# Last batch of a memory-attention kernel: result rows staged in four buffers, and the last head's share added to a result prepared without it

## What is computed

```python
xn = layernorm(x)
# attention memory: 8 heads, chunks of 64 tokens, weights updated by scanned gradients
vals = silu(q @ (mem_w0 + updates0)) @ (mem_w1 + updates1)      # per head, 128 wide
vals = rmsnorm(vals) * (mh_gamma + 1.0) * sigmoid(sr @ w_gate)  # scale per token and head
s = (vals of all heads side by side) @ w_combine                # a sum over heads
# top-1 expert of 8 for each token
ffn = relu(xln @ w1[e] + b1[e]) @ w2[e] + b2[e]
g = silu(xn + alpha * ffn)
out = x + s * g                                                 # s is shifted by 63 tokens
```

## Time and profile before

| | us |
|---|---|
| median of 3 runs | 1113.71 |
| lowest and highest run | 1113.23, 1114.35 |
| the profiled execution: its own time | 1113.32 |
| its span, first to last instruction | 1110.8 |
| mean granted TensorE clock in the span, share of full speed | 0.987 |

### The profile page before, as it was taken

The page is one execution under the profiler, slowest core; times in us unless marked ns, Lnnn a source line. Parts: engine busy times, 40 slices in busy tenths (PEclk is TensorE's granted clock), DMA queues, the critical chain, the costliest instruction groups (busy, mean ns, idle before and its releaser), DMA issues. The chain is left out here.

```text
span 1110.8 us, 19052 instructions
## 1 busy us (share of the span) xinstructions
PE 1071.7 (96%) x6613; PEld 900.1 (81%) x6613; DVE 686.0 (62%) x1752; ACT 678.7 (61%) x1356; POOL 562.4 (51%) x574
## 2 busy tenths in 40 slices
PE   6899799999999999999999999999999999999994
PEld 4666588888888888888888888888888888888883
DVE  5887566767766555565556555565556555657774
ACT  5776466677655656565556555665566565656663
POOL 6885244478874444344434444444434443444553
PEclk9999699999999999999999999999999999999997
DMA  7210300000030000000000000000000000012221
GB/s 205 79 46 29 105 1 1 1 15 30 21 97 12 19 10 9 8 21 10 9 8 11 20 11 8 9 20 11 8 8 11 20 8 6 6 42 61 69 70 42
DMA packets 42129, 32.66 MB, mean 29 GB/s; under 512 B 4042, under 2 KB 36652, under 8 KB 41900
## 3 DMA queue, kind: packets, MB, share of 16 engines
q1 hardware_dynamic: 38484, 25.93, 8.0%
q0 software_dynamic: 2304, 4.74, 1.3%
q10 hardware_dynamic: 1248, 0.79, 0.2%
HBM read 18.30 MB, written 13.41 MB: 29 GB/s over the span
## 5 line engine op out<-in xcount | busy, mean ns | idle before, releaser
L1040 DVE TENSOR_TENSOR p_sb<-bank,coef 128x512 f32<-128x512 f32 (+3 forms) x512 | 218.8, 483 | 3.1 <-PE bank L749 2.6
L1232 POOL TENSOR_TENSOR sq_rest<-sq,sq_high 128x450 f32<-128x450 f32 x64 | 67.2, 1050 | 245.1 <-ACT sq_high L934 245.1
L772 PE MATMUL bank<-p_sb,err_t 128*128 128x450 f32 (+3 forms) x512 | 132.9, 402 | 0.2 <-DVE p_sb L1040 0.2
L772 PE MATMUL bank<-p_sb,du_t 128*128 128x450 f32 (+3 forms) x512 | 128.8, 394 | 0.0
L772 PEld LDWEIGHTS bank<-p_sb,err_t 128*128 128x128 f32 x512 | 83.7, 190 | 45.5 <-DVE p_sb L1040 25.2
L1236 POOL TENSOR_TENSOR sq_low<-sq_rest,sq_mid 128x450 bf16<-128x450 f32 x64 | 67.6, 1056 | 96.5 <-ACT sq_mid L948 96.2
L772 PEld LDWEIGHTS bank<-p_sb,du_t 128*128 128x128 f32 x512 | 82.1, 190 | 41.4 <-issue 23.9
L1093 DVE SCALAR_TENSOR_TENSOR acc<-bank,rg,acc 128x128 f32<-128x128 f32 x224 | 62.9, 343 | 68.2 <-POOL rg L1220 68.2
L1118 DVE SCALAR_TENSOR_TENSOR du<-q_sb,bank 128x512 f32<-128x512 f32 x64 | 44.0, 688 | 87.7 <-PE bank L749 87.7
L1216 POOL TENSOR_TENSOR rs<-ms,neg_half 128x4 f32<-128x4 f32 x64 | 80.6, 1259 | 28.6 <-DVE ms L1075 27.3
L1207 POOL TENSOR_TENSOR s_low<-s_sb,s_high 128x512 fp32r<-128x512 f32 x64 | 82.7, 1293 | 20.2 <-ACT s_high L911 20.1
(11 more groups left out here) (297 smaller groups left out, 3103.1 us busy)
## 6 DMA issues: line engine op xcount, KB each, us to landing
sorted_rows<-coef SPq DMA_DIRECT2D x5, 516.0 KB, 5.0
rows<-sorted_rows SPq DMA_DIRECT2D x40, 64.5 KB, 1.8
x<-in_L_attn_inputs SPq DMA_DIRECT2D x8, 256.0 KB, 5.5
x_rows<-x SPq DMA_DIRECT2D x8, 256.0 KB, 2.3
ew<-in_L_ffn_w SPq DMA_DIRECT2D x8, 256.0 KB, 3.9
attn_out<-acc SPq DMA_DIRECT2D x7, 256.0 KB, 2.1
ew<-attn_out SPq DMA_DIRECT2D x7, 256.0 KB
ew<-ffn_rows SPq DMA_DIRECT2D x8, 192.0 KB
```

Source lines behind the costliest of these rows:

```text
L772: last = pe.matmul(out[:, P * i:QW], rows[:, i, :], p_sb[:, P_COL[i]:P_COL[i] + QW - P * i], start=False, stop=True, skip_group_check=True)
L1040: last = nc.vector.tensor_tensor(dst, src, w, ALU.mult)
L1232: nc.gpsimd.tensor_tensor(sq_rest[:], sq[:], sq_3[0][:], ALU.subtract).then_inc(g_rest, 1)
```

## The change

Five edits, all in `attend`:

1. Four sets of `fin_f`, `fin_x`, `fin_o` in place of two. The odd ones lie in the space of the first expert weights. Semaphores and SP's loop follow: sets 0 to 3 are loaded one behind the other, and set c after result c-4 has been stored.
2. The work on them is placed anew. `SUMMED` says whose `last_sum` comes at the end of which head's step: batch h in head h up to 2, batches 3 and 4 in head 3, then 5, 6, 7 in heads 4, 5, 6, none in head 7. `gate_rows` and POOL's product come in the next head's step, at its end as before (a first of two ahead of `vals`); `add_rows` comes one head later still, and in the middle of the step, between `err_low` (L1115) and `du` (L1118).
3. In the last head's step the squares are not split into three bf16 parts: TensorE multiplies the fp32 `sq` by a column of ones in fp32, four products.
4. In the last head's step VectorE makes batch 7's result but for its last head's share, and `finish` then adds that share alone, in two halves. SP stores the result by two transfers, and ScalarE's queue issues the third.
5. The five operations on the token factors become `shares()`, called at the end of head 2's step.

The diff, cut to its core:

```diff
@@ -30,6 +30,8 @@
...
 X_FIRST, X_LAST = 2, 6
+FINS = 4
+SUMMED = [(0,), (1,), (2,), (3, 4), (5,), (6,), (7,), ()]
@@ -678,7 +680,8 @@
...
         late = carve(m.ew2[:].rearrange("p e k d -> p (e k d)"), [0])
-        fin_f, fin_x, fin_o = ([late(T, D) for k in range(2)] for _ in range(3))
+        later = carve(m.ew1[:].rearrange("p e d -> p (e d)"), [0])
+        fin_f, fin_x, fin_o = ([(late, later)[k % 2](T, D) for k in range(FINS)] for _ in range(3))
@@ -729,9 +732,13 @@
...
-        def last_head(s):
-            return s[1] if s is not None and s[0] == B - 1 else None
+        def summed(s):
+            if s is None or s[0] < B - 1:
+                return (), ()
+            return SUMMED[s[1]], SUMMED[s[1] - 1] if s[1] else ()
+        final = lambda s: s == (B - 1, H - 1)
@@ -862,8 +869,13 @@
...
                             pe.matmul(VB[0:r, t * P:t * P + P], vals[:, t * P:t * P + r], m.w_out[:, s[1], :], start=True, stop=True)
-                        pe.wait_ge(g_lo, k + 1)
-                        for t, r in enumerate(Q_ROWS):
+                        if final(s):
+                            pe.wait_ge(a_sq, k + 1)
+                            for t, r in enumerate(Q_ROWS):
+                                last = pe.matmul(QA[0:r, SUMS + t:SUMS + t + 1], sq[:, t * P:t * P + r], m.ones[:, 0:1], start=True, stop=True)
+                        else:
+                            pe.wait_ge(g_lo, k + 1)
+                        for t, r in enumerate(() if final(s) else Q_ROWS):
@@ -924,6 +936,9 @@
...
                         nc.scalar.copy(err_2[0][:], err[:]).then_inc(a_eh, 1)
+                    begun = summed(s)[1]
+                    for c in begun if final(s) else begun[:-1]:
+                        gate_rows(c)
@@ -931,7 +946,8 @@
...
                         act.wait_ge(a_sq, k + 1)
-                        nc.scalar.copy(sq_3[0][:], sq[:]).then_inc(a_hi, 1)
+                        if not final(s):
+                            nc.scalar.copy(sq_3[0][:], sq[:]).then_inc(a_hi, 1)
@@ -943,12 +959,11 @@
...
                         nc.scalar.copy(du_t[:].rearrange("p t d -> p (t d)"), EB[:]).then_inc(a_dt, 1)
-                    if s is not None:
+                    if s is not None and not final(s):
...
                         nc.scalar.copy(sq_3[1][:], sq_rest[:]).then_inc(a_mid, 1)
-                    c = last_head(s)
-                    if c is not None and c > 0:
-                        gate_rows(c - 1)
+                    if begun and not final(s):
+                        gate_rows(begun[-1])
@@ -959,7 +974,8 @@
...
                     if f is None and s is None:
-                        gate_rows(B - 1)
+                        act.wait_ge(v_o, B + 1)
+                        act.dma_start(out[B - 1, SHIFT + (T - 1) * P:S, :], fin_o[(B - 1) % FINS][0:Q_LAST - 1, T - 1, :]).then_inc(s_res[(B - 1) % FINS], 16)
@@ -1020,6 +1036,9 @@
...
                     nc.vector.tensor_copy(m.xl_all[:, :, D].bitcast(I32), m.token_i[:]).then_inc(v_placed, 1)
+                def shares():
@@ -1085,6 +1104,9 @@
...
                             dve.wait_ge(v_acc, l)
+                    if final(z):
+                        finish()
+                    elif z is not None:
@@ -1113,6 +1135,10 @@
...
                         nc.vector.tensor_tensor(err_2[1][:], err[:], err_2[0][:], ALU.subtract).then_inc(v_el, 1)
+                    for c in summed(z)[1]:
+                        if c < B - 1:
+                            add_rows(c)
+                    if f is not None:
@@ -1131,6 +1157,8 @@
...
                             coefs(1)
+                        if k == 2:
+                            shares()
@@ -1140,18 +1168,15 @@
...
                         dve.wait_ge(m.s_scatter, 16 * NT)
-                    c = last_head(s)
-                    if c is not None:
+                    for c in summed(s)[0]:
                         last_sum(c)
-                        if c > 0:
-                            add_rows(c - 1)
-                    if s is None and f is None:
-                        finish_batch()
+                    if final(s):
+                        attention_before_last_head()
...
-                    q = c % 2
-                    dve.wait_ge(s_fin[q], 16 * 5 * (c // 2 + 1) if c < B - 1 else 16 * (5 * 3 + 4))
+                    q = c % FINS
+                    dve.wait_ge(s_fin[q], 16 * 5 * (c // FINS + 1) if c < B - 1 else 16 * (5 + 4))
@@ -1159,19 +1184,30 @@
...
                 def add_rows(c):
-                    q = c % 2
+                    q = c % FINS
...
-                def finish_batch():
-                    q = (B - 1) % 2
+                def attention_before_last_head():
+                    q = (B - 1) % FINS
                     dve.wait_ge(a_g, B)
-                    dve.wait_ge(v_acc, B * H)
-                    dve.wait_ge(s_res[q], 32 * ((B - 1) // 2))
+                    dve.wait_ge(v_acc, B * H - 1)
+                    dve.wait_ge(s_res[q], 32 * ((B - 1) // FINS))
+                    link(nc.vector.tensor_tensor(fin_o[q], acc[:], fin_f[q], ALU.mult))
+                    link(nc.vector.tensor_tensor(fin_o[q], fin_o[q], fin_x[q], ALU.add))
+                def finish():
+                    q = (B - 1) % FINS
                     for k in range(2):
+                        for t in range(2 * k, 2 * k + 2):
+                            r = Q_ROWS[t]
+                            share = fin_f[q][0:r, t, :]
+                            last = nc.vector.scalar_tensor_tensor(share, VB[0:r, t * P:t * P + P], rg[0:r, t:t + 1], share, ALU.mult, ALU.mult)
+                        link(last)
                         part = lambda t: t[:, 2 * k:2 * k + 2, :]
-                        link(nc.vector.tensor_tensor(part(fin_o[q]), part(acc[:]), part(fin_f[q]), ALU.mult))
-                        nc.vector.tensor_tensor(part(fin_o[q]), part(fin_o[q]), part(fin_x[q]), ALU.add).then_inc(v_o, 1)
+                        nc.vector.tensor_tensor(part(fin_o[q]), part(fin_o[q]), part(fin_f[q]), ALU.add).then_inc(v_o, 1)
@@ -1244,10 +1280,9 @@
...
                         nc.gpsimd.indirect_dma_start(m.ffn_rows, bass.IndirectOffsetOnAxis(ids[r][:, 0:1], axis=0), y[r], None).then_inc(s_y[r], 16)
-                    c = last_head(s)
-                    if c is not None and c > 0:
-                        q = (c - 1) % 2
-                        pool.wait_ge(a_g, c)
+                    for c in summed(s)[1] if not final(s) else ():
+                        q = c % FINS
+                        pool.wait_ge(a_g, c + 1)
@@ -1276,15 +1311,15 @@
...
                 def parts(c):
-                    q = c % 2
+                    q = c % FINS
...
                 def result(c, k=None):
-                    q, src = c % 2, fin_o[c % 2]
-                    for t0, t1 in ((0, T - 1), (T - 1, T)) if k is None else (((0, 2),) if k == 0 else ((2, 3), (3, 4))):
+                    q, src = c % FINS, fin_o[c % FINS]
+                    for t0, t1 in ((0, T - 1), (T - 1, T)) if k is None else ((2 * k, 2 + k),):
@@ -1314,20 +1349,21 @@
...
                 for c in range(B):
-                    if c >= 2:
-                        sp.wait_ge(v_o, c - 1)
-                        result(c - 2)
-                        sp.wait_ge(s_res[c % 2], 32 * (c // 2))
+                    if c >= FINS:
+                        sp.wait_ge(v_o, c - FINS + 1)
+                        result(c - FINS)
+                        sp.wait_ge(s_res[c % FINS], 32 * (c // FINS))
...
                     parts(c)
-                sp.wait_ge(v_o, B - 1)
-                result(B - 2)
+                for c in range(B - FINS, B - 1):
+                    sp.wait_ge(v_o, c + 1)
+                    result(c)
...
                     result(B - 1, k)
-                sp.wait_ge(s_res[0], 32 * B // 2)
-                sp.wait_ge(s_res[1], 32 * B // 2 + 16)
+                for q in range(FINS):
+                    sp.wait_ge(s_res[q], 32 * (B // FINS) + (16 if q == (B - 1) % FINS else 0))
```

More of the change, by code:

```diff
@@ L713, in attend @@
         s_y = [sem(f"s_y{k}") for k in range(RING)]
-        s_fin, s_res = ([sem(f"{n}{k}") for k in range(2)] for n in ("s_fin", "s_res"))
+        s_fin, s_res = ([sem(f"{n}{k}") for k in range(FINS)] for n in ("s_fin", "s_res"))
         v_f, a_g, g_o, v_o = sem("v_f"), sem("a_g"), sem("g_o"), sem("v_o")
@@ L882, in gate_rows @@
                         n = c * T + t
-                        last = nc.scalar.activation(fin_f[c % 2][:, t, :], fin_f[c % 2][:, t, :], ACT.Silu, bias=token_q[:, 1, n:n + 1], scale=token_q[:, 2, n:n + 1])
+                        last = nc.scalar.activation(fin_f[c % FINS][:, t, :], fin_f[c % FINS][:, t, :], ACT.Silu, bias=token_q[:, 1, n:n + 1], scale=token_q[:, 2, n:n + 1])
                     last.then_inc(a_g, 1)
```

## The result

The changed kernel takes 1105.39 us (median of 5 runs, 1102.08 to 1106.67), the kernel before beside it on the same chip 1113.79 (5 runs, 1113.23 to 1114.4). The ratio is 0.992, with a 95% interval of 0.9903 to 0.9936: 8.4 us less, faster, and inside the predicted range of 1104.7 to 1107.6. The profiled execution took 1105.39, with a span of 1103.6, where the kernel before had 1113.32 and 1110.8. So 7.2 us went out of the span, and another 0.7 lies around it (own time less span: 2.5 before, 1.8 after). Lines named here are lines of the changed kernel, and in the experiments of the kernel that was run.

A forecast was written before the change was run, and what follows sets the result against it. TensorE, busy 96% of the span, was taken as the bound. Terms 1.0 + 0.9 + 0.6 + 4.3 + 0.8 + 0.1 = 7.7 us off 1113.32 gave 1105.6, plus 0.39 for the runs' median: 1106.0, range 1104.7 to 1107.6.

The forecast's parts named there:

- Step ends in batch 7: Steps behind heads 1, 2, 5 recover 0.34 us each, heads 3 and 4 stay late; 1.0 us won, bounds 0 to 1.7.
- Token factors: Batch 0: without the five operations at the step's end, ms comes earlier; 0.9 us won, bounds 0.6 to 1.0.
- Start of the last head's step: TensorE waits there for xs_low behind a late ms; all 0.61 comes back: 0.6 us won, bounds 0.5 to 0.65.
- Squares in fp32: Last head's step: vals to ms shrinks from 6.99 to 2.65 us; 4.3 us won, bounds 3.0 to 5.2.
- The last share: Kernel's end: last additions to last add take 2.07 us instead of 2.89; 0.8 us won, bounds 0.6 to 0.9.
- The last transfers: Kernel's end: two issuers let the last transfers end sooner; 0.1 us won, bounds −0.5 to 0.35.
- Step ends stay late: Rival: double sums or POOL hold ms in all five steps of batch 7; 6.7 us won, 1107.0 us; chance 0.11.
- all of them recover: Rival: all step ends recover, last sums being faster; +0.7, 1105.3 us, with cheaper squares 1104.7; chance 0.11.
- the fp32 sums slow: Rival: last head's fp32 sums run at 1.2 GHz or cost double; 1.0 to 1.3 us less won, 1107.2; chance 0.07.
- the prepared result in the way: Rival: in the last step ms queues on VectorE behind the result's preparation; the 4.3 goes, 1110.3 us; chance 0.02.
- Slower: the loads of sets 4 to 7: Rival: last_sum waits for loads that need a stored result, ms behind it; 13.2 us cost, 1119.2 us; chance 0.03.

The follow-up runs named there:

- Experiments 4: The changed kernel with the last head's squares in three bf16 parts again, the rest kept: 1107.37 us, ratio 0.9935.
- 7: The kernel before with only the last head's squares taken in plain fp32: one run, 1111.69 us beside 1111.6 for the kernel before.
- Experiments 1: The changed kernel with one small product on POOL after its last work, which nothing waits for: 1107.79 us, ratio 0.9945.
- 3: The changed kernel with the last head added before products and adds again, and SP issuing all three transfers: 1105.53 us, ratio 0.9924.
- experiment 8: The changed kernel with the last head's root on ScalarE, its reciprocal and product on VectorE, off POOL: one run, 1101.96 us beside 1111.6.
- 11: 10 with the last head added before products and adds again: 1102.38 us, ratio 0.9908.
- 10: The changed kernel with the last head's rs and rg off POOL, one last_sum per head's step, and SP issuing the third transfer: 1102.85 us, ratio 0.9904.
- experiment 6: The changed kernel with three sets of result buffers instead of four: one run, 1111.07 us beside 1111.6 for the kernel before.
- experiment 5: The changed kernel with POOL's product of result rows moved to the middle of the next step: one run, 1107.35 us beside 1111.6.

## Why the prediction was right, and where it was wrong

| term | predicted | measured, us |
|---|---|---|
| Step ends in batch 7 | 1.0 | 1.2 |
| Token factors | 0.9 | 0.86 |
| Start of the last head's step | 0.6 | 0.60 |
| Squares in fp32 | 4.3 | 4.5 |
| The last share | 0.8 | 0 |
| The last transfers | 0.1 | 0 |
| sum | 7.7 | 7.1 (span: 7.2) |

From the first projection to the end it is 985.9 us before and 978.5 after, 7.4 less. The 0.2 beyond the terms lies spread over steps that no edit touches. The token factors and the start of the last head's step have no run of their own; they are read from the rows.

*Step ends in batch 7.* Right in kind: behind heads 1, 2 and 5 all came back, behind heads 3 and 4 not. The four steps took 56.26 us and take 55.40, and `w1n` in the fifth is 0.34 earlier: 1.2. Mis-sized was the step behind head 3, for which I had a loss of 0.48 against 0.34; it lost 0.31 (14.04 less 13.73). `ms` was 0.59 late and not 0.75: the eight operations ended 14.56 us after the step's start (1046.42 − 1031.86), where I had 14.7, and `ms` starts while the last one runs out. Behind head 4 the loss is 0.21, where 0.23 was predicted, and by the mechanism predicted. `ms` there is on time and takes its usual 0.16 us (1059.78), while POOL's product runs from 1057.94 to 1060.55. This agrees with the Trainium skill, "SBUF — State Buffer", section "Who interferes with whom", by which a VectorE instruction with at most one SBUF input, outside its two-port modes, doesn't contend with GpSimd.

*Token factors, Start of the last head's step.* Right. The latter is 15.66 − 14.72 = 0.94, less the 0.34 already counted.

*Squares in fp32.* Right in mechanism and nearly in size. Eight fp32 records with one column took 0.85 us, where I had taken 1.0 from L864; at full clock, with no gap ahead. The way from `vals` to `ms` took 2.52; the prediction has 2.65 for it, while its own terms add up to 2.63. Experiments 4 and 7 show the part that the term's name hides: with `add_rows` still ahead of `ms`, 2.3 of the 4.5 would have stayed (4.82 against 2.52).

*The last share, The last transfers.* Here the prediction failed. "From the last head's addition at 1104.67 to the end of the last add (1107.14 + 0.42) pass 2.89 us" is right, and it did become 2.05 (2.07 forecast; the terms given there, with the overlap, add up to 2.00). The step that failed is the one that I took without saying it: that the span ends with the landing of the last data, so that an earlier last add is an earlier end. In both kernels it ends with POOL's drain, 6.4 us from `rg`. The profile before had the sign: SP had its result landed at 1109.50, 1.3 us before the end, and then waited 1.1 for another engine. Experiments 1, 3 and 8 show it, and 11 against 10 shows the 0.8 us that the share is worth when the drain is moved away. So the size of that term was right and the path wrong. The last transfers did land earlier, their data by 0.2 us and SP's wait by 0.1, also without effect on the end. So 0.9 of the 7.7 were credited to edits that brought nothing.

*Why the time was nearly hit nonetheless.* By the measured terms the profiled execution would have taken 1113.32 − 7.1 = 1106.2; it took 1105.39. All but 0.1 of the rest lies around the span: 2.5 us in the profiled execution before, 1.8 after. In 28 further executions of the kernel before this part is 1.7 to 3.6 us, with a median of 1.9, and in the 11 of the changed kernel it is 1.8. So most of the 0.7 is the chance of which execution was profiled. It made up for the 0.9 that the tail did not give: the mechanism of four terms was right, and that the total came this near was in part luck.

*The rivals.* "Step ends stay late" and "all of them recover" are both excluded by the steps, "the fp32 sums slow" by 0.85 us at a clock of 1.00, "the prepared result in the way" by `ms` waiting 1.82 us for TensorE. "Slower: the loads of sets 4 to 7" doesn't occur with four sets, and does with three (experiment 6).

## What to carry to other kernels

Before you credit an edit at the very end of a kernel, find what ends the span: look for time between the last wait on a landing and the last instruction, and on which engine the last work began. If POOL has a small operation late in the tail, as here, try it on another engine first: here that brought 2.1 us, and only then did a faster result count (0.8). And when a chain has two ways in, as `ms` had, cut both in one go: here either alone brought 2.2 or 1.8 of the 4.5.

## What the runs showed of the hardware that was not expected

- POOL's closing DRAIN ends 5.95 to 5.97 us after the end of POOL's last instruction, in all 14 traces. Its record takes in that instruction: 6.19 to 6.21 us where it took 0.2, 7.43 to 7.44 where it took 1.28. At the end of the program's first block the record is 2.2 us. Why it is so long wasn't tried.
- VectorE under POOL's work: the four operations of a `last_sum`, each with two inputs in SBUF, took 1.14 us with POOL idle, 1.92 with one POOL operation inside them and 2.92 with more, and `err_low` 1.75 instead of 0.68 in experiment 5.
- The ScalarE table for Sqrt took 1.28 us to load, which costs nothing where ScalarE is idle (experiment 8).
- The steps of batch 7 repeat to 0.03 us from one trace of the same code to the next, and the other steps of the heads to 0.14, but for one first step (15.4 against 14.6). Most of the scatter comes from the stage ahead of them (122.7 to 126.2 us).
